# Where the second half of the output projection's weights is split

## The reference

```
sa, ca, ga, sb, cb, gb = six vectors from silu(c) @ wmod        # ga, gb kept away from 0
h = layernorm(x) * (1 + ca) + sa
x = x + ga * (attention(h) @ Wo)      # 32 query heads, 8 key heads, head size 64, rotary, causal
h = layernorm(x) * (1 + cb) + sb
x = x + gb * ffn(h)                   # weights rounded to ternary in groups of 64, silu gate, rms norm
```

## Time and profile before

| what | value |
|---|---|
| median of 3 runs | 1734.54 us (1732.52 to 1736.47) |
| the profiled execution, its own time | 1730.82 us |
| its span, first to last instruction | 1729.0 us |
| mean granted TensorE clock | 0.994 |
| PE busy / DVE / ACT / POOL | 97% / 72% / 66% / 57% of the span |
| last group of heads ends, first piece of the projection starts | 1159.57 us |
| chunk 1 of the projection starts | 1212.36 us |

### The profile page before, as it was taken

The page is one execution under the profiler, slowest core; times in us unless marked ns, Lnnn a source line. Parts: engine busy times, 40 slices in busy tenths (PEclk is TensorE's granted clock), DMA queues, the critical chain, the costliest instruction groups (busy, mean ns, idle before and its releaser), DMA issues. The chain is left out here.

```text
span 1729.0 us, 27586 instructions
## 1 busy us (share of the span) xinstructions
PE 1675.4 (97%) x8993; PEld 1386.7 (80%) x8993; DVE 1248.8 (72%) x2518; ACT 1140.5 (66%) x2315; POOL 977.1 (57%) x822
## 2 busy tenths in 40 slices
PE   6899999999999999999999999889999899999998
PEld 2588888888888888888888888667788688888886
DVE  6788889888889888888888988873333564545433
ACT  4588888888888888888888888863232443323222
POOL 1367777777777777777677777445000245444453
PEclk9999999999999999999999999999999999999999
DMA  7234444445445354454354454456555101001000
GB/s 295 71 106 118 131 122 124 122 112 137 112 117 142 99 132 126 103 139 128 96 148 114 107 132 126 132 152 203 188 187 173 53 1 31 25 13 43 0 31 25
DMA packets 174969, 190.92 MB, mean 110 GB/s; under 512 B 31456, under 2 KB 117736, under 8 KB 174832
## 3 DMA queue, kind: packets, MB, share of 16 engines
q1 hardware_dynamic: 137840, 140.99, 28.7%
q10 hardware_dynamic: 36992, 48.25, 10.2%
HBM read 86.12 MB, written 31.74 MB: 68 GB/s over the span
## 5 line engine op out<-in xcount | busy, mean ns | idle before, releaser
L1102 DVE TENSOR_TENSOR p_lo<-ps_b,p_hi 128x512 fp32r<-128x512 f32 x576 | 395.1, 688 | 103.3 <-ACT p_hi L987 99.5
L987 ACT CAST p_hi<-ps_b 128x512 fp32r<-128x512 f32 x576 | 338.2, 589 | 116.3 <-PE ps_b L889 87.7
L1002 ACT ACTIVATE p<-ps_b,negm 128x640 f32<-128x640 f32 (+7 forms) x512 | 382.9, 752 | 41.2 <-DVE negm L1113 39.8
L1113 DVE CUSTOM_DVE_ANT_0 ps_b<-ps_b,mask_w 128x640 f32<-128x640 f32 (+7 forms) x512 | 385.4, 760 | 21.6 <-PE ps_b L878 17.6
L889 PE MATMUL ps_b<-ident,p 128*128 128x128 f32 x2304 | 345.6, 274 | 9.2 <-DVE p_lo L1102 9.1
L889 PEld LDWEIGHTS ps_b<-ident,p 128*128 128x128 f32 x2304 | 271.9, 140 | 56.1 <-DVE p_lo L1102 13.4
L877 PE MATMUL ps_b<-k_hh,q_hl 128*128 128x512 f32 (+3 forms) x768 | 265.6, 347 | 7.5 <-ACT p L1002 6.8
L903 PE MATMUL ps_b<-p_hi,v_hl 128*128 128x512 f32 x576 | 257.9, 448 | 4.0 <-ACT o_sb L995 3.5
L878 PE MATMUL ps_b<-k_l,q_hl 128*128 128x512 f32 (+3 forms) x768 | 256.2, 347 | 0.0
L904 PE MATMUL ps_b<-p_lo,v_hl 128*128 128x512 f32 x576 | 226.6, 393 | 0.0
L1741 PE MATMUL ps_d<-h_hi,gu 128*128 128x512 f32 x512 | 200.6, 392 | 2.4 <-DVE h_lo L1861 2.4
(11 more groups left out here) (160 smaller groups left out, 3123.6 us busy)
## 6 DMA issues: line engine op xcount, KB each, us to landing
rot_x<-rot_s SPq DMA_DIRECT2D x320, 64.0 KB, 2.0
q_hl<-rot_s SPq DMA_DIRECT2D x128, 128.0 KB, 2.6
q_hl<-rot_x SPq DMA_DIRECT2D x128, 128.0 KB, 2.8
rd_all<-reciprocals SPq DMA_DIRECT2D x128, 128.0 KB, 3.0
o_low<-o_sb ACTq DMA_DIRECT2D x128, 128.0 KB, 2.3
attention_out<-o_sb SPq DMA_DIRECT2D x128, 128.0 KB, 2.5
o_raw<-attention_out SPq DMA_DIRECT2D x32, 512.0 KB, 4.7
wf<-in_L_ffn_w_gate_up ACTq DMA_DIRECT2D x28, 256.0 KB, 3.1
```

Of the source, the lines that this page charges most:

```text
L987: act.copy(p_hi[:, T % P_RING, :], ps[:, T_BANK + T % 2, :]).then_inc(phi_ready, 1)
L1002: act.activation(p_32[:, parity, h, column * P:column * P + nk], s, ACT.Exp, bias=negm[:, k:k + 1], scale=-1.0, accum_out=den[:, parity, k ...
L1102: dve.tensor_tensor(p_lo[:, T % P_RING, :], ps[:, T_BANK + T % 2, :], p_hi[:, T % P_RING, :].bitcast(F32), ALU.subtract).then_inc(plo_read ...
L1113: dve.tensor_tensor_reduce(s, s, mask_w[:, S - nk:S], 1.0, HIGHEST, ALU.add, ALU.min, negm[:, k:k + 1]).then_inc(max_ready, 1)
```

## The change

Weights 0 to 3 stay in the last group of heads. Weights 4 to 7 are cast and subtracted at the head of chunk 0 of the output projection: on ACT behind the loads of unit 2 and of the ternary weights and ahead of the absolute value of unit 2, on DVE ahead of the sum of unit 2. The loads of weights 4 and 5 stay at steps 45 and 48 of the last group; the loads of weights 6 and 7 go to the head of SP's list of chunk 0, ahead of the load of piece 4. On PE each of the pieces 0 to 3 waits for its own two weights, where piece 0 waited for all eight.

```diff
+WO_HERE = 4
@@ SP, last group
-                for i in range(2, 8):
+                for i in range(2, WO_HERE + 2):
                     if at == SP_REST and at_last(body, T, WO_NEXT[i - 2]):
                         outputs.load_weights(sp, i)
@@ ACT, last group
-                for i in range(8):
+                for i in range(WO_HERE):
                     if at == ACT_REST and at_last(body, T, WO_HIGH[i]):
@@ SP, output projection
         def body(n, first):
+            for i in range(WO_HERE + 2, 8 if first else 0):
+                load_weights(sp, i)
             for s in range(NPC):
@@ PE, output projection
-                if first and s == 0:
-                    pe.wait_ge(wo_ready, 2 * PH)
+                if first and i == 0:
+                    pe.wait_ge(wo_ready, 2 * (p + 1))
@@ ACT, output projection
             load_tern(n, 1)
+            for i in range(WO_HERE, 8 if first else 0):
+                weights_high(act, i)
@@ DVE, output projection
         def body(n, first):
+            for i in range(WO_HERE, 8 if first else 0):
+                weights_low(dve, i)
```

## The result

The changed kernel takes 1741.21 us (median of 14 runs, 1732.70 to 1744.34), the kernel before beside it 1732.45 us (14 runs, 1730.80 to 1738.96). The ratio is 1.0036 with a 95% interval of 1.0022 to 1.0050: 4 to 9 us slower. It is not the ratio of the two medians, which is 1.0051; the means of the runs are 6.1 us apart, the medians 8.8. Run once more on another occasion the ratio was 1.0029 (1.0017 to 1.0040). The time lies in the range, and the sign is as forecast. The profiled execution took 1735.32 us, 4.5 more than that of before; the forecast was 4.1. It was the third fastest of the 14, 5.9 us under their median.

The account below looks back on a forecast made before the run. PE, busy 97% of the span, was taken to bound the kernel. A 7.1 us later chunk 1 less 3.0 us gained in the last group gives +4.1 on 1734.54: 1738.6 us, range 1733.0 to 1743.0.

Parts of the forecast that it names:

- The waits by piece bring nothing: Projection start: the last weight is subtracted 7 us before PE arrives, so waiting piece by piece gains nothing by itself.
- The chain through ACT, DVE and POOL sets the pace of chunk 0: Chunk 0: rounding the units already sets PE's pace; PE waits 2.2 us ahead of piece 3 and 1.7 ahead of chunk 1.
- Steps 1 to 4: Head of chunk 0: splits, POOL's slip of 0.86 us and late loads delay the sum of unit 2 by 9.7 us.
- step 3: Head of chunk 0: weights 6 and 7, loaded behind the last store, land at 1170.5 and 1172.2 while ACT stands still.
- Step 5: Ahead of piece 2: its o_lo comes late, so PE starts at 1179.2, not 1170.89, a new wait of 8.3 us.
- Step 6: Unit 3: a short landing of unit 2's store gains 2.6 us at the pick, leaving the units' chain at +7.1 us.
- Steps 7 and 8: Piece 3 starts 8.1 us later; the low clock falls in piece 2 instead, leaving PE at +6.5 us from piece 4.
- The rule on idle time: A PE that idles between blocks starts each throttled again; by it piece 3 would be slow again.
- Step 9: Chunk 1 starts on the later of PE, +6.5 us, and the units' chain, +7.1: 7.1 us later, all reaching the end.
- The last group, +3.0: Attention's tail: removing 4 casts and 4 subtractions cuts PE's waits by 3.0 us, bounds 0 to 4.9.
- the prediction's own signs: Wrong if piece 2 starts without a long wait, the first piece comes forward under 2 us, or chunk 1 starts before 1212.
- the first rival: Chunk 0: unit 2's store again takes 4.9 us, or piece 3 starts at 1.2 GHz; +6.7, 1741.2 us; chance 0.13.

Follow-up runs that it names:

- the kernel with the clock kept up: Changed kernel with 28 more 128x512 matmuls on PE between piece 1 and the wait of piece 2; ratio to before 1.0031.
- the half-moved kernel: Changed kernel with only weights 6 and 7 split at the head of chunk 0 and all loads in the last group; ratio to before 0.9998.
- the late splits: Changed kernel with the splits of weights 6 and 7 put behind the split of piece 2, their loads still behind the last store; ratio to before 1.0000.
- the weights left out: Changed kernel with weights 4 to 7 neither loaded, cast nor subtracted, PE waiting for the first four only; ratio to before 0.9976.

## Why the prediction was right, point by point

- *The waits by piece bring nothing:* shown, 0.9997 with them alone.
- *The chain through ACT, DVE and POOL sets the pace of chunk 0:* shown by the kernel with the clock kept up, where a quicker piece 2 wins nothing.
- *Steps 1 to 4, the head.* ACT casts 4 and 5 in its idle time, stands still for the landing, and the sum of unit 2 comes later on the axis of piece 0: forecast 9.7, measured 15.07 - 5.32 = 9.75. The POOL division was put at 2.14 us and took 2.16. The two subtractions beside it took 3.66 us and not 2.4; the sum did not have that term, and it is hidden there by the landing. It is not hidden in the half-moved kernel.
- *The size of the landing in step 3.* It was put at 3.7 us and took 4.1, and ACT stood still for 6.55 us where some 5 were expected. The figure of 2.0 us that the prediction sets beside it from the Trainium skill ("DMA: Bandwidth & Descriptors", section "Anatomy of one DMA") is given there for DMAs that GpSimd issues, while SP issues these; the sum did not use it.
- *Step 3 is the main cost.* Loads at the head or not, with two splits in both: 1.0036 against 0.9998, 6.6 us. This pair changes nothing else, and shows it. With four splits, with the landing or without, it is 1.0029 to 1.0036 against 0.9990. With the late splits the wait follows the landing to piece 3. What is left for the four splits is 2.4 us by the runs (0.9990 against 0.9976) and 4.5 by chunk 0 of the two traces (57.4 against 52.9). In the changed kernel the loads of 6 and 7 could not have been early: `wo_raw` has two slots, and weights 4 and 5 hold them until they are subtracted at the head.
- *Step 5:* a new wait of 8.3 us ahead of piece 2; measured 7.65 and 7.56.
- *Step 6, the landing of unit 2's store:* the pick of unit 3 waits 0.37 us, for POOL, and not 3.23. Right, in both traces.
- *Steps 7 and 8:* piece 3 was put 27.8 us behind piece 0 and came 27.95 and 27.82 behind. In the first trace that is by another path than forecast: not `o_lo` was last, but piece 2 itself. Its 24 matmuls took 8.2 us at a clock of 0.64 where the sum had 7.2. In the second trace `o_lo` was last, with 0.69 us of wait. Piece 3 then ran at the full clock, as forecast; the first trace:

```profile
1177.00:1185.20 8.20, 8.20 (x24) 6.37 (x24) 2.31 (x3) 3.12 (x4) 5.23 (x6) 0.64 0.51 172
...
1185.20:1191.20 6.00, 6.00 (x33) 4.84 (x32) 3.16 (x3) 3.11 (x4) 3.89 (x4) 1.00 0.46 153
```

- *The rule on idle time that the prediction set beside step 8* (the Trainium skill, "TensorE: Matmul & The Clock Gate", section "HAM oscillation"): its example has longer waits than the 2.22 and 1.7 us on which the prediction tried it. In these traces waits of about 2 to 3 us were followed by the low clock in some places and not in others, and both waits of over 7 us were.
- *Step 9:* +7.1 from piece 0 to chunk 1. The two traces have 58.3 and 60.2 us against 52.0 to 54.4 where nothing was moved, +6.1 between the means. One term scattered: the pick of unit 5 waited 4.13 us for a landing before, and then 2.92 in the first trace and 5.19 in the second:

```profile
1205.15 0.69 DVE L1158 SCALAR_TENSOR_TENSOR w_hat<-gscale,w_abs 128x512 bf16<-128x512 bf16 x1 [2.92 <-DMA ternary<-w_hat]
```

```profile
1206.45 0.69 DVE L1158 SCALAR_TENSOR_TENSOR w_hat<-gscale,w_abs 128x512 bf16<-128x512 bf16 x1 [5.19 <-DMA ternary<-w_hat]
```

- *The last group, +3.0.* Too large for the first trace: there the stretch is only 0.9 us shorter, and the clock fell to 1.2 GHz at 1145 to 1152. Held against the traces of before that have the same low stretch (122.3 and 122.4), it is 1.7 to 1.8 shorter; without such a stretch it is 2.9 in the second trace and 2.5 with the weights left out. Timed runs with the weights left out say 4.2 (2.8 to 5.7). The bounds 0 to 4.9 held; what the sum lacked is a term for the clock. By the prediction's own signs this was a warning: it called itself wrong if the first piece came forward by less than 2 us, and in the first trace it came forward by 1.83 (in the second by 2.6).

The net of +4.1 came close to the profiled execution's +4.5 in part by luck. There the last group gave 0.9 and not 3.0, chunk 0 took 5.5 and not 7.1, the stretch ahead of the last group was 1.0 shorter and the rest 0.9 longer. For the runs the net was low: +5.0 to +6.2 by the two ratios, +8.8 by the medians of the first occasion. That 1738.6 lies only 2.6 us under the measured 1741.21 is luck as well: it started from the median of three runs, 1734.54, and the median of the kernel before was then 1732.45. The measured median is also the number of the first rival, 1741.2. Neither of its mechanisms is in the two traces, since the pick of unit 3 found its store landed and piece 3 ran at the full clock; for the slower executions, which have no trace, it is not excluded.

What the excess of the runs is made of stays open. The head costs 9 to 10 us in timed runs and about 6 in the two traces. The changed kernel runs at a lower mean clock (0.989 against 0.992), which would be up to some 5 us by an estimate from these two clocks and the span; but the kernel with the clock kept up had 0.992 and was no faster, so the clock alone doesn't explain it.

## What to carry to other kernels

A load that was hidden by the distance between its issue and its use must be moved with that distance, or not at all: with two splits at the head, moving their loads behind the last store cost 7 us. All four splits at the head, without a landing, cost 2 us in the runs. Before work is put at the head of an in-order list, look for which idle time behind it in the same list is long enough, and for what the first item of the list feeds; here the gap stood one step later, behind piece 2. A net that comes out right may hold terms that missed both ways, so compare stage by stage, with more than one trace of each kernel. And a gain of a few us in a part bound by several engines at once should be given with the spread of the clock in it.

## What was not expected of the hardware

- DVE's subtraction of 128x1024, 1.22 us alone, takes up to 2.31 us beside a POOL operation, and the POOL operation goes from 1.28 to 2.16 us. In the prediction only POOL was to slow down. The trace of the kernel before had it already, in a row that the prediction did not use, beside a POOL operation of 2.21 us:

```profile
1189.93 2.18 DVE L1390 TENSOR_TENSOR o_lo<-o_raw,o_hi 128x1024 fp32r<-128x1024 f32 x1
```

- A load of 512 KB took 4.1 us in the changed kernel and 8.8 us when the loads of gates and rows, 768 KB on ACT's queue, were under way at the same time.
- The same wait of PE can be followed by the low clock or not: 3.10 us of idle by a clock of 1.00, 1.96 us by 0.57.
- The kernel before against itself gave a ratio of 0.9990 with an interval of 0.9978 to 1.0002, and once 0.9999. Under 0.1% one ratio doesn't settle a verdict here.
